# Scale rows sent once per 32 partitions and spread by VectorE, in the first stage of a decoder block on one core

## What is computed

```
def _mxfp4_matmul(x, codes, scales, block_size=32):
    w = codes * jnp.repeat(scales, block_size, axis=0)
    return x @ w
q = _mxfp4_matmul(x, wq_codes, wq_scales) + bq     # 256 -> 2048, k and v alike
...
attn = softmax(q k^T / sqrt(128));  out = attn v
return _mxfp4_matmul(out, wo_codes, wo_scales) + bo   # 2048 -> 256
```

## Time and profile before

| | us |
|---|---|
| median of 3 runs | 637.88 |
| lowest and highest | 635.74, 640.84 |
| profiled execution, span from first to last instruction | 630.6 |
| PE busy in the span | 567.4 (90%) |
| DVE busy | 394.2 (63%) |
| POOL busy | 196.6 (31%) |
| DMA queue of SP and ACT (q1), share of 16 engines over the span | 33.5% |

### The profile page before, as it was taken

One profiled execution on the slowest core, in us unless ns is written; L12 is line 12 of the kernel. 1 busy time (PEld: TensorE's weight loads), 2 busy tenths in 40 slices (PEclk: granted clock), 3 DMA queues, 4 the chain that ended last, 5 costly groups with the idle time before them and its releaser, 6 DMA issues.

```text
span 630.6 us, 10511 instructions
## 1 busy us (share of the span) xinstructions
PE 567.4 (90%) x3751; PEld 468.2 (74%) x3751; DVE 394.2 (63%) x923; ACT 249.9 (40%) x515; POOL 196.6 (31%) x169
## 2 busy tenths in 40 slices
PE   6879998999999979999989989898899889999950
PEld 5669887898888979566566757565688777999940
DVE  3565756627454565976486465788777589655527
ACT  1325635536464534001122121044524568666630
POOL 4614441003000010422152413413617724444440
PEclk9779999999999989999999999899989999999985
DMA  8999914005030022999200000050106394344318
GB/s 233 264 221 220 230 41 167 0 2 183 2 126 2 1 98 78 346 317 331 78 1 1 0 2 1 0 223 35 68 13 247 105 309 143 107 113 124 114 22 312
DMA packets 25121, 76.93 MB, mean 122 GB/s; under 512 B 4839, under 2 KB 11631, under 8 KB 24432
## 3 DMA queue, kind: packets, MB, share of 16 engines
q1 hardware_dynamic: 19264, 62.33, 33.5%
q0 software_dynamic: 3792, 8.43, 3.8%
q10 hardware_dynamic: 2016, 5.50, 2.8%
HBM read 66.77 MB, written 28.48 MB: 151 GB/s over the span
## 4 chain that ended last, share of the span: by engine, by line
PE 58%; DVE 17%; issue 9%; DMA 7%; POOL 6%; ACT 2%; SPq 1%; POOLq 0%; DVEq 0%; ACTq 0%
PE psum L690 8%; PE psum L559 7%; PE psum L708 6%; PE psum L859 5%; PE psum L624 5%; DMA sclB<-in_scl 5%; PE psum L611 5%; PE psum L572 4%; DVE tt L1260 3%; POOL rows_of_experts L1640 3%; PE psum L752 2%; PE psum L603 2%; DVE EW L1468 2%; PE psum L590 1%; PE psum L675 1%
## 5 line engine op out<-in xcount | busy, mean ns | idle before, releaser
L1260 DVE TENSOR_TENSOR tt<-psum,tab 128x512 f32<-128x512 f32 x96 | 60.8, 682 | 33.7 <-PE psum L690 33.1
L1612 POOL TENSOR_TENSOR rp<-tt,tt 128x512 f32<-128x512 f32 x24 | 30.7, 1278 | 109.0 <-DVE tt L1260 109.0
L559 PE MATMUL psum<-xTh,W 128*128 128x512 f32 x128 | 54.9, 429 | 9.3 <-DVE W L1160 7.4
L708 PE MATMUL psum<-rp,Mb 128*128 128x512 f32 x128 | 57.8, 597 | 0.3 <-DVE rp L1285 0.3
L859 PE MATMUL psum<-EW,xgh 128*128 x188 | 56.7, 344 | 0.5 <-issue 0.4
L1646 POOL DMA_INDIRECT parts_of_tokens<-yb,xg x39 | 40.4, 1035 | 51.4 <-ACT yb L1093 51.1
L1230 DVE TENSOR_TENSOR OTl<-psum,OTh 128x512 fp32r<-128x512 f32 x32 | 22.1, 691 | 54.3 <-ACT OTh L960 54.3
L559 PE MATMUL psum<-xTl,W 128*128 128x512 f32 x128 | 53.6, 418 | 0.0
L993 ACT ACTIVATE qP<-psum 128x512 f32<-128x512 f32 x16 | 9.6, 598 | 96.0 <-PE psum L708 96.0
L690 PE MATMUL psum<-xTh,Ah 128*128 128x512 f32 x96 | 42.3, 441 | 4.4 <-DVE ex_la L1340 2.3
L708 PEld LDWEIGHTS psum<-rp,Mb 128*128 128x128 f32 x128 | 24.0, 192 | 26.4 <-issue 25.6
(11 more groups left out here) (254 smaller groups left out, 1530.7 us busy)
## 6 DMA issues: line engine op xcount, KB each, us to landing
rows_of_experts<-in_empty SPq DMA_DIRECT2D x8, 2064.0 KB, 32.0
exr<-in_ex SPq DMA_DIRECT2D x9, 608.0 KB, 6.4
xg<-rows_of_experts SPq DMA_DIRECT2D x39, 129.0 KB, 2.2
exr<-in_ex ACTq DMA_DIRECT2D x7, 608.0 KB, 5.0
raw<-in_codes SPq DMA_DIRECT2D x4, 1024.0 KB, 20.4
sclB<-in_scl SPq DMA_DIRECT2D x16, 256.0 KB, 12.1
yv<-parts_of_tokens SPq DMA_DIRECT2D x8, 512.0 KB, 7.1
raw<-in_codes SPq DMA_DIRECT2D x4, 512.0 KB, 17.3
```

Of the source, the lines that this page charges most:

```text
L559: mm = pe.matmul(ap, W[:, kt, m, 512 * hq + 128 * h:512 * hq + 128 * h + 128], xp[:, kt, 512 * g:512 * g + 512], start=(n == 0), stop=(n = ...
L708: mm = pe.matmul(ap, Mb[:, 4 * hp + 2 * kk + half_, :], rp[(j0 + kk) % 3][:, half_, :], start=(n == 0), stop=(n == 3))
L1260: return tt_(b3(tt[n][:, :], 64), b3(src, 64), tab[:, j % 3, n, :].unsqueeze(1).to_broadcast([128, 8, 64]), ALU.mult)
L1612: tt_(o[:, 0, :], tt[0][:, :], tt[1][:, :], ALU.subtract).then_inc(s_rp_lo, 1)
```

## The change

Scales. Each scale row is now loaded to one partition of 32 (`sclB[0:128:32, ...]`), one DMA for q and k, one for v and one for wo. A DVE step `scales(hq, k)` then copies the first partition of each 32 to the other 31, in place, by `stream_shuffle`; k = 0 is q and k, 1 is v, 2 is wo. For quarter 0 the q and k scales are spread in two halves. `sclB` and `wob` are set to zero once ahead of it, one part by DVE and three by POOL ahead of POOL's other memsets. `raw` and `sclB` are laid out by matrix first, then by half of the input.

First quarter. The q and k codes come in two DMAs of two heads each, and the product is made by four DVE instructions, one per head, two of them between the turns of the normalised tiles. The second `warm(30)` becomes `warm(8)`, behind those turns. The wo product of quarter 0 goes from DVE to POOL.

Order of the later quarters. `scales(c + 1, 1)`, `weights_v(c + 1)`, `scales(c + 1, 2)` and `weights_wo(c + 1)` stand where `weights_vo(c + 1)` stood. `scales(c + 2, 0)` and `weights_qk(c + 2)` stand after `turn(c, 3)`. Quarter 1's q and k product goes ahead of `v(0, ...)`.

Constants. The tables, the output bias, the context and its sine table, and the second half of x move from ACT's queue or the head of SP's queue to later places in SP's queue, and some semaphores are joined.

```diff
 def stage_order():
-    yield from [("norm", 0, (0, 1, 2, 3)), ("center", 0, (0, 1, 2, 3)), ("warm", 30)]
-    yield from [("norm_turn", 0, t) for t in range(4)]
-    yield from [("warm", 30), ("weights_qk", 0), ("weights_vo", 0), ("load_w", 1)]
+    yield from [("scales", 0, 0, 0), ("norm", 0, (0, 1, 2, 3)), ("center", 0, (0, 1, 2, 3)), ("warm", 30)]
+    yield from [("norm_turn", 0, 0), ("norm_turn", 0, 1), ("weights_qk", 0, 0), ("norm_turn", 0, 2), ("norm_turn", 0, 3)]
+    yield from [("weights_qk", 0, 1), ("scales", 0, 0, 1), ("weights_qk", 0, 2), ("weights_qk", 0, 3)]
+    yield from [("warm", 8), ("scales", 0, 1), ("weights_v", 0)]
+    yield from [("scales", 0, 2), ("weights_wo", 0), ("load_w", 1)]
     yield from [("qk", 0, h) for h in range(4)]
-    yield ("context",)
+    yield from [("scales", 1, 0), ("weights_qk", 1, None), ("context",)]
     for i in range(4):
         yield from [("v", 0, i), ("v_out", 0, i)]
     for c in range(8):
-        if c == 0:
-            yield ("weights_qk", 1)
...
         if c < 3:
-            yield ("weights_vo", c + 1)
+            yield from [("scales", c + 1, 1), ("weights_v", c + 1), ("scales", c + 1, 2), ("weights_wo", c + 1)]
         if c < 2:
-            yield from [("load_w", c + 2), ("weights_qk", c + 2)]
+            yield ("load_w", c + 2)
         for i in range(6):
             if i < 4:
                 yield ("turn", c, i)
+            if i == 3 and c < 2:
+                yield from [("scales", c + 2, 0), ("weights_qk", c + 2, None)]
...
+            nc.vector.memset(sclB[:, 0:2, :, 0:256], 0.0).then_inc(s_clean, 1)
+
+            def scales(hq, k, piece=None):
+                part_ = (sclB[:, 0:2, :, :], sclB[:, 2:3, :, :], wob[:, :, :])[k]
+                if piece is None:
+                    ve.wait_ge(d_scl[k], 16 * (hq + 1))
...
+                nc.vector.stream_shuffle(part_, part_, [0] * 32).then_inc(s_scl, 1)
...
             def load_w(hq):
...
-                    for r in range(4):
-                        dma(sclB[32 * r:32 * r + 32, :, a:b, :],
-                            scl[hq, r][:, a:b, :].partition_broadcast(32)).then_inc(d_scl[k], 16)
...
+                sp.wait_ge(*wqk(hq - 1, 3))
+                scales_in(hq, 0)
+                sp.wait_ge(*wv(hq - 1))
+                scales_in(hq, 1)
+                sp.wait_ge(*wo_(hq - 1))
+                scales_in(hq, 2)
                 dma(wor[:, :, :], woc[hq]).then_inc(d_wor, 16)
-                for r in range(4):
-                    dma(wob[32 * r:32 * r + 32, :, :], wos[hq, r].partition_broadcast(32)).then_inc(d_wor, 16)
```

More of the change, by code:

```diff
@@ L343, in program @@
         MF = ofs[0]
-        raw = [at(f"raw{i}", MF + 12288 * i, [128, 2, 3, 512]) for i in range(2)]
+        raw = [at(f"raw{i}", MF + 12288 * i, [128, 3, 2, 512]) for i in range(2)]
         Mb = at("Mb", MF, [128, 32, 128])
@@ L537, in warm @@
             def warm(n):
-                te.wait_ge(s_ident, 1)
+                te.wait_ge(s_ident, 2)
                 for _ in range(n):
@@ L1521, in finish @@
                     tt_(xs[:, t, :], yv[t][:, 1, :], xs[:, t, :], ALU.add).then_inc(s_y, 1)
-            part = {"norm": norm, "center": center, "norm_turn": norm_turn, "weights_qk": weights_qk, "weights_vo": weights_vo, "qk": qk,
-                    "v_out": v_out, "scores": scores, "probs": probs, "values": values, "bias": bias, "rows": rows,
+            part = {"norm": norm, "center": center, "norm_turn": norm_turn, "scales": scales, "weights_qk": weights_qk,
+                    "weights_v": weights_v, "qk": qk, "v_out": v_out, "scores": scores, "probs": probs, "values": values, "bias": bias, "rows": rows,
                     "query_weights": query_weights, "rotate": rotate, "gate": gate, "cross_scores": cross_scores,
@@ L1647, in block_down @@
                                              in_offset=None, bounds_check=4 * 1024 - 1, oob_is_err=False).then_inc(d_yb[b % NX], 16)
-            part = {"norm": norm, "context": context, "weights_qk": weights_qk, "weights_vo": weights_vo,
-                    "probs": probs, "bias": bias, "rotate": rotate, "split13": split13, "split2": split2,
+            part = {"norm": norm, "context": context, "weights_qk": weights_qk, "weights_v": weights_v,
+                    "weights_wo": weights_wo, "probs": probs, "bias": bias, "rotate": rotate, "split13": split13, "split2": split2,
                     "low": low, "scatter": scatter, "block_down": block_down}
@@ L1660, in sync_program, with scales_in @@
             dma = nc.sync.dma_start
[L1662 to L1677 removed]
+            def scales_in(hq, k):
+                to, of = ((sclB[0:128:32, 0:2, :, :], scl[hq][:, 0:2, :, :]), (sclB[0:128:32, 2:3, :, :], scl[hq][:, 2:3, :, :]),
+                          (wob[0:128:32, :, :], wos[hq]))[k]
+                dma(to, of).then_inc(d_scl[k], 16)
@@ new lines, in load_w @@
+            def load_w(hq):
+                if hq >= 2:
+                    sp.wait_ge(*wv(hq - 2))
+                dma(raw[hq % 2][:, 0:2, :, :], codes[hq][:, 0:2, :, :]).then_inc(d_raw[hq % 2][0], 16)
+                if hq == 1:
+                    dma(kvr[:, :, :], kvc).then_inc(d_kvr, 16)
+                    dma(cksb[:, :, :], cks).then_inc(d_kvr, 16)
+                dma(raw[hq % 2][:, 2:3, :, :], codes[hq][:, 2:3, :, :]).then_inc(d_raw[hq % 2][1], 16)
+                if hq == 1:
+                    dma(xs[:, 4:8, :], x[:, 4:8, :]).then_inc(d_x[1], 16)
+                sp.wait_ge(*wqk(hq - 1, 3))
[4 more added lines that the diff above has]
+                scales_in(hq, 2)
```

142 lines of the change are left out of this document (73 added, 69 removed).

## The result

The changed kernel took 651.99 us (median of 4 runs, 650.93 to 652.89) against 639.07 us for the kernel before (4 runs, 635.74 to 640.84): ratio 1.0208, interval 1.0175 to 1.0241. It is slower by 12.9 us. The forecast was 645.3, its range ended at 650. The profiled execution took 651.23 us, 1.3 us more than its span of 649.9; over all runs on record a time is 1.2 to 2.5 us above its span. So what lies around a span is not 7.3 us. The execution profiled for before (span 630.6) would have taken about 632 us, some 4 us less than the fastest of its four runs.

What follows compares the result with a forecast made beforehand. The prediction took DMA as the bound early and PE from about 40 us on. Its terms -4.9 + 3.6 + 2.6 + 6.1 = +7.4 us gave a 638.0 us span; with 7.3 us outside, 645.3 (range 636.5 to 650).

Steps and rivals of the forecast that it cites:

- Part 2: After qk(c + 1), kT, DVE's shuffle and POOL's product precede PE's v: PE idles 3.7 us per quarter, three times.
- The terms c = 1 and c = 2: Waits before v(2, 0) and v(3, 0): +3.6 us, and +2.6 us as the v product no longer meets xh.
- the first term of the sum: Start to v(1, 0): it comes at about 46.3 instead of 51.2, a gain of 4.9 us (3 to 10).
- The contention: Quarter 1's q and k product on DVE, slowed beside POOL's work: ready at 32 us (26.2 to 33.5).
- the second product is ready before 29 us: Sign of being wrong: quarter 1's q and k product ready before PE asks for it at 29 us.
- The clock term: Behind PE's gaps before v(1, 0), v(2, 0), v(3, 0): half speed, 2.0 us lost each, +6.1 us (0 to 9).
- The 7.3 us between span and median: Time outside the profiled span, added to the forecast span of 638.0 to give 645.3 us.
- rival 5: Start: scale DMAs to four partitions land slowly, second product at 36 us, +4 us, 649; chance 0.05.
- rival 4: Shuffle costs more (2.3 us): +1.1 in each of three waits, 1 to 2 early; 649 to 650; chance 0.10.
- Rivals 1: PE's clock holds in most gaps, at most one drop: 639 to 641 us; chance 0.15.
- rival 3: PE starts early and its clock survives the gaps: faster, 631.5 to 634 us; chance 0.10.
- Rival 2: Early part: quarter 1's product does not meet POOL, v(1, 0) at 41: +2.3 us, 640; chance 0.14.

Runs made afterwards that it cites:

- e5: The kernel before, profiled once more with no edit: 638.36 us, ratio 1.0013.
- e6: The changed kernel, run and profiled again with no edit: 651.97 us, ratio 1.0216.
- e9: The kernel before, profiled a third time with no edit, on a third chip: 628.92 us, beside one run of before at 630.09.
- e10: The changed kernel, profiled a third time with no edit, on a third chip: 647.17 us, beside one run of before at 630.09.
- e2: Changed kernel with `context` moved ahead of quarter 0's wo product in POOL's queue: 646.42 us, ratio 1.0143.
- e3: Changed kernel with 24 identity turns on PE in each gap ahead of v(1), v(2) and v(3): 643.85 us, ratio 1.0107.
- e8: Changed kernel with each v scale shuffle of quarters 1 to 3 made twice: 655.12 us (one run).
- e1: Changed kernel with the v scales' shuffle and v product a step earlier, behind those of q and k: 632.11 us, ratio 0.9921.
- e4: Changed kernel with both the v shuffle and product a step earlier and `context` ahead of quarter 0's wo product: 624.57 us, ratio 0.9807.
- e7: The order of e4, with scales broadcast by DMA to 32 partitions again and shuffles cut to 2 or 4 elements: 636.71 us, ratio 0.997.

## Why the prediction was wrong

**The direction and the mechanism of the new wait held.** Part 2 named the chain `kT`, shuffle, POOL's product, v, and its gap of 3.7 us per quarter: measured 3.72, 4.04 and 4.83. The terms c = 1 and c = 2 were 3.6 and 2.6; against the first execution of before, the steps from v(1) to v(2) to v(3) grew by 30.2 - 24.5 = 5.7 and 29.7 - 25.2 = 4.5 us, the clock included. Forecast with the clock: 5.6 and 4.6. Against that one execution the whole sum was close: scores(3) came 8.7 us later (122.8 for 114.1) where +7.4 was forecast. What failed is that its early part did not stand for the kernel whose median was forecast.

**The step that failed is the first term of the sum, "a gain of 4.9 us stands at this point".** v(1) came at 48.0, not 46.3, and the point that it was measured from stood at 46.3 and 45.4 in the two other executions of before, not at 51.2. So the head start was not -4.9 but +1.7 (against e5). With e5 as the kernel before, the loss reads, up to scores(3):

| stretch | e5 | after | difference |
|---|---|---|---|
| start to v(1) | 46.3 | 48.0 | +1.7 |
| v(1) to v(2) | 26.3 | 30.2 | +3.9 |
| v(2) to v(3) | 25.2 | 29.7 | +4.5 |
| v(3) to scores(3) | 13.2 | 14.9 | +1.7 |
| sum | 111.0 | 122.8 | +11.8 |

Between the two medians lie 12.9 us, and between e5 and e6 11.7 us of span, so the part before scores(3) holds all of the loss but about 1 us. Of the pair e9 and e10 it holds less: 14.5 of 18.3 us of span, one execution each. Two things made this term wrong:
- The baseline. The prediction credited the change with the removal of a slow stretch of 6 us at a granted clock of 0.50 that one execution of before had and two others had not (2.6 us of the 4.9), and with scales that landed 2.3 us later there than in e5. The term should have been taken from qk(1)'s release with a clock of either level.
- A wait that the prediction does not have. It followed `context` on POOL only as a rival of DVE's product. But `context` uses the softmax's own buffer `sm` as scratch (line 1579 writes it, line 1586 reads it), so DVE waits for the last `kv` before the first softmax. With the wo product of quarter 0 moved to POOL and ahead of it, `context` ends at 34.0 in place of 29.25. The prediction had PE wait from 29 to 32 us for weights; PE waited from 32.4 to 38.05 for PSUM. e2 shows it: with only that order changed, v(1) comes 6.5 us earlier.

**The contention was mis-costed.** The product of quarter 1 was to be ready at 32, of which 6.6 us were taken from the price of line 1168 (to 30.5); it ended at 26.70 (24.01 + 2.69), close to the lower end, 26.2. That "the second product is ready before 29 us" was named as a sign of being wrong, and it came. What was won there was lost again to `context`. The slowing is not proportional (last section).

**The clock term was too large.** +6.1 was taken; e3 gives 3.5 us with the third gap partly covered. The loss behind a gap was right in kind (0.50, 0.58, 0.50), but the 2.0 each came from full stretches; 1.4 was measured for each of the first two. What the prediction and the expectations call 1.2 and 2.4 GHz is in the windows a granted clock of 0.50, with a matmul of 512 columns in 0.43 us (12 in 5.16 us, 1.2 columns a ns), and of 1.00, with one in 0.2135 us (20 in 4.27 us, 2.4 columns a ns). This error is part of why the steps of c = 1 and c = 2 fit so well: their waits were longer than the 3.7 us taken, 4.04 and 4.83.

**The base.** The 7.3 us between span and median was an accident of one execution (1.3 us around a span here). Added to its span it still gave the median of before, so it did no harm by itself. But the first execution was 3.1 us behind e5 at scores(3) and 8.8 us ahead of it from there on, and the terms were read from the part that was behind.

**The miss of 6.7 us in terms.** Head start +6.6. Step of c = 1 with its clock 3.9 for 5.6 forecast: -1.7, since in e5 the step before the change was 26.3 and not 24.5. Step of c = 2: -0.1. The stretch behind v(3), all clock in the forecast, 1.7 for 2.1: -0.4. Together +4.4. The other 2.3 us are the median of before (639.1 for 637.9) and 1.1 us between the two medians that scores(3) does not show.

**What was right as forecast.** The shuffle (1.2 and 2.3 us taken) measured 1.28 to 1.38 and 2.47 to 2.62 over all kernels that have it in full. Norm began at 6.04 (6.5), qk(0) at 12.77 (13.2), POOL was free at 7.7 (7.9). The memsets, the moved constants and the shuffles between two OTl cost nothing: between 10 and 123 us PE's waits are the three shown. The scale DMAs to four partitions were no trouble (2.91 us of DVE's wait at the start, rival 5 ruled out), and the shuffle took 1.3 us, not the 2.3 of rival 4; e8 shows what a second one costs, its own 1.3 us in each wait. Rivals 1 and 3, a clock that holds, fell with the windows, though e1 and e4 do show the head start of rival 3 once the waits are gone. Rival 2 had its condition fulfilled (a product at 26.2, measured 26.70), but not its v(1) at 41.

**Open.** Why the last 520 us of the same kernel differ by up to 9 us between executions is not settled, but the traces show where. The first matmul of the shared expert (line 783, 790 in the changed kernel) comes 334.9 to 335.6 us behind scores(3) in the three executions of before and 337.2 to 338.0 in the three of the changed kernel. The first turn of an expert's product (line 871, 878) follows 58.3, 66.9 and 59.6 us after it in before, e5 and e9, and 67.0, 65.5 and 59.7 in after, e6 and e10. From there to the end all six take 122.2 to 122.9. So the spread of each kernel arises almost wholly in one stretch of some 60 us. In it PE stands for 2.4 us with no releaser in e5, after and e6, and not in the others. Both executions on the third chip are among the short ones, so chip and chance are not separated. The 2 us by which the changed kernel is later at line 790 have no cause shown either. All this limits what a single span can tell here, and is why the account above ends at scores(3).

## What to carry to other kernels

A step put into an in-order queue inherits every wait ahead of it: placed behind `kT`, a 1.3 us shuffle and the product that waits for it cost 3.7 to 4.8 us of PE three times, and placed a step ahead it cost nothing (652.0 against 632.1 us). When work is moved onto an engine, follow what is behind it there to its last consumer, scratch buffers included: a 2.4 us product moved ahead of `context` stopped DVE, ACT and PE one after the other. And take a head start from more than one execution of the kernel before, since two executions of it differed at v(1) by 4.9 us, as much as the whole gain that was forecast there.

## What the runs showed of the hardware

**DVE's and POOL's products took turns, instruction by instruction.** The times fit one engine standing until the other's instruction ends, and not both going slower. In the timeline of the changed kernel the quarter 1 product starts at 24.01 and takes 2.69 us, 0.40 more than alone (2.29): POOL's `kvt` ends at 24.55, and the product ends 2.15 us after that. POOL's next pair, begun at 24.51, takes 4.57 us; in e7, where no DVE product stands beside it, it takes 2.50. In e4 POOL's `kv`, beside the quarter 1 product (24.11, 2.51 us), takes 6.80 against 4.82 here. In e4 the v product of quarter 0 meets `kvt`:

```profile
16.09 2.40 POOL L1579 TENSOR_TENSOR kvt<-kvr,cksb 128x1024 f32<-128x1024 f32 x1 [5.98 <-DMA cksb<-in_cks]
...
17.16 2.41 DVE L1188 TENSOR_TENSOR W<-raw,sclB 128x1024 fp32r<-128x1024 f32 x1
18.45 3.54 POOL L1581 TENSOR_TENSOR sm<-kvr,cksb 128x512 f32<-128x512 f32 x2
```

`kvt` ends at 18.49; the product then needs 1.08 us to its end at 19.57, near the 1.23 that it takes alone in the changed kernel. By this reading line 1168 of before (3.29 us, 1.18 alone) and the `xh` of the earlier trace rows (3.13 us, 1.0 alone) were one wait of 2.1 us each for a POOL instruction, and not slow work. The forecast's 6.6 us for a product "wholly beside POOL" did not occur. The longest that a product of 2048 elements took on DVE is 4.38 us, in e7: it starts 0.11 us behind POOL's wo product, which ends at 37.03, and ends 2.15 us after that, so its loss is that one POOL instruction.

**The shuffles were not held by POOL.** In e4 the shuffle of 2048 elements takes 2.58 us at 21.43, across POOL's `sm` and `kv` products, and in e1 2.58 us at 49.98, with POOL idle. Over all kernels, shuffles of this size took 2.47 to 2.58 us with POOL idle and 2.58 to 2.62 us beside it. So the prediction's estimate for it, taken from OTl's 0.69 us beside POOL, held.
